# Relative tags early in each fourth step, the second edge bias added by VectorE, the n gate's h half behind the edge transposes

## The reference, cut to what matters

```python
edge_index = jnp.stack([src, dst])
h = jnp.maximum(_layernorm(x, axis=-1), 0.0)
# messages: each edge through the two-layer network of its type
msg_input = jnp.concatenate([h[src], h[dst]], axis=1)
for t in range(n_types):
    a = jax.nn.relu(msg_input @ W1[t] + b1[t])
    m = a @ W2[t] + b2[t]
    msgs = msgs + jnp.where((edge_type == t)[:, None], m, 0)
agg = jax.ops.segment_sum(msgs, dst, num_segments=num_nodes)
# a GRU cell on every node
gi = agg @ W_ih.T + b_ih
gh = h @ W_hh.T + b_hh
r = jax.nn.sigmoid(i_r + h_r)
z = jax.nn.sigmoid(i_z + h_z)
n = jnp.tanh(i_n + r * h_n)
out = x + (1.0 - z) * n + z * h
```

## Time and profile before

| | before |
|---|---|
| median of 3 runs | 1806.55 us (1804.4 to 1809.14) |
| the profiled execution | 1805.01 us, of it 1803.1 in the span |
| TensorE products busy | 1631.5 us (90%) |
| VectorE busy | 1592.3 us (88%) |
| ScalarE busy | 1460.1 us (81%) |
| GpSimd busy | 1235.9 us (69%) |
| TensorE's mean granted clock | 0.98 of full speed |

### The profile page before, as it was taken

How to read it: one execution, slowest core, us unless ns; L and a number is a source line. 1 busy time by engine, 2 the same in 40 slices (tenths; PEclk the granted TensorE clock), 3 DMA queues, 4 the chain that set the end, 5 groups by cost and what they waited for, 6 DMA issues and landing times.

```text
span 1803.1 us, 43100 instructions
## 1 busy us (share of the span) xinstructions
PE 1631.5 (90%) x10182; PEld 1428.9 (79%) x10182; DVE 1592.3 (88%) x4186; ACT 1460.1 (81%) x3401; POOL 1235.9 (69%) x1982
## 2 busy tenths in 40 slices
PE   0226799999999999999999999999999999999998
PEld 0115688888888888888888888888888888888887
DVE  8597699888989898898899999999999999999886
ACT  0025788888888888888888999989989999899895
POOL 4777777777777777777776676666767667676420
PEclk9985899999999999999999999999999999999999
DMA  2224677777777777777777777777777777777653
GB/s 70 50 46 125 166 191 194 195 188 192 193 195 193 194 197 188 188 188 191 193 190 196 195 195 199 193 197 197 196 198 194 199 199 192 200 193 197 182 145 96
DMA packets 477071, 319.72 MB, mean 177 GB/s; under 512 B 106705, under 2 KB 463009, under 8 KB 476962
## 3 DMA queue, kind: packets, MB, share of 16 engines
q10 hardware_dynamic: 261792, 156.12, 28.6%
q1 hardware_dynamic: 185730, 106.99, 25.9%
q0 software_dynamic: 29440, 55.47, 12.8%
HBM read 211.65 MB, written 106.72 MB: 177 GB/s over the span
## 4 chain that ended last, share of the span: by engine, by line
PE 77%; POOL 6%; issue 4%; DVE 2%; ACT 1%; POOLq 0%; ACTq 0%; DVEq 0%
PE bank L1332 14%; PE bank L1334 13%; PE bank L1333 13%; PE bank L1412 10%; PE bank L1424 4%; PE bank L1423 4%; PE bank L1440 4%; PE bank L1450 4%; PE bank L1402 4%; PE bank L1394 4%; POOL e_x L580 3%; DVE n_sel L1071 2%; PE bank L1436 1%; POOL lists L566 1%; ACT e_h L1177 0%
## 5 line engine op out<-in xcount | busy, mean ns | idle before, releaser
L580 POOL DMA_INDIRECT e_x<-in_x,rows_now x816 | 852.5, 1045 | 237.4 <-issue 220.5
L1177 ACT ACTIVATE e_h<-e_x,shift,rstd 128x128 f32<-128x128 f32 x816 | 355.4, 485 | 117.3 <-DVE shift L1048 93.3
L1194 ACT ACTIVATE n_h<-n_x,shift,rstd 128x128 f32<-128x128 f32 x784 | 385.0, 492 | 0.1
L1071 DVE TENSOR_SCALAR n_sel<-iota,n_rel 128x256 fp32r<-128x256 f32 x784 | 233.1, 359 | 37.6 <-POOL n_rel L631 35.7
L1412 PE MATMUL bank<-n_sel,n_win 128*128 128x256 f32 x1568 | 235.0, 292 | 31.0 <-DVE n_sel L1071 31.0
L1332 PE MATMUL bank<-n_h_hi,whh_hi 128*128 128x512 f32 x588 | 247.8, 421 | 2.9 <-ACT n_zc L1285 2.6
L1332 PE MATMUL bank<-n_a_hi,wih_hi 128*128 128x512 f32 x588 | 249.5, 424 | 0.9 <-DVE bank L1083 0.9
L1333 PE MATMUL bank<-n_h_lo,whh_hi 128*128 128x512 f32 x588 | 233.0, 396 | 0.0
L1334 PE MATMUL bank<-n_a_hi,wih_lo 128*128 128x512 f32 x588 | 232.6, 396 | 0.0
L1334 PE MATMUL bank<-n_h_hi,whh_lo 128*128 128x512 f32 x588 | 232.4, 395 | 0.0
L1333 PE MATMUL bank<-n_a_lo,wih_hi 128*128 128x512 f32 x588 | 232.1, 395 | 0.0
(11 more groups left out here) (179 smaller groups left out, 3757.7 us busy)
## 6 DMA issues: line engine op xcount, KB each, us to landing
n_win<-messages SPq DMA_DIRECT2D x1568, 64.2 KB
messages<-e_msg ACTq DMA_DIRECT2D x204, 257.0 KB, 3.1
n_x<-in_x ACTq DMA_DIRECT2D x195, 256.0 KB
out<-n_out ACTq DMA_DIRECT2D x195, 256.0 KB
e_x<-in_x,rows_now POOLq DMA_INDIRECT x816
rows_now<-lists SPq DMA_DIRECT2D x204, 2.0 KB, 3.0
lists<-picks,list_rows POOLq DMA_INDIRECT x72, 2.9
w<-in_W SPq DMA_DIRECT2D x1, 512.0 KB, 4.9
```

The source lines that it names most:

```text
L580: G.indirect_dma_start(e_x[:, s, 2 * end + t, :], None, x, bass.IndirectOffsetOnAxis(ap=rows_now[:, s, t, end:end + 1], axis=0)).then_inc( ...
L1071: ins = V.tensor_scalar(n_sel[:, s % 2, k, :], iota[:], n_rel[:, s % 2, k:k + 1], None, ALU.is_equal)
L1177: last = A.activation(e_h[:, s % 2, k, :], e_x[:, s, k, :], ACT.Relu, scale=rstd[:, slot, col + k:col + k + 1], bias=shift[:, slot, col + ...
L1194: last = A.activation(n_h[:, s % 2, cols], n_x[:, s, cols], ACT.Relu, scale=rstd[:, slot, col + 4 + k:col + 5 + k], bias=shift[:, slot, co ...
```

## The change

Four edits. (1) GpSimd makes `n_rel` in steps with m mod 4 = 2, the ones behind the inverse roots, ahead of the gate and of all four gathers instead of behind the second. (2) TensorE's product of ones with the bias rows goes, and the products with `w2` start the bank themselves. Instead the bias is laid out once over all partitions as `b2_all` (ScalarE copies it in step 7 out of `bank[BIN]`, where an existing product has put it), and VectorE adds it in each step: `e_m` = bank + `b2_all`, behind n_e, for unit i-9. (3) So ScalarE makes the high half from `e_m`, in SBUF, one step later than before (unit i-10), behind the first two `e_h`; VectorE takes `e_m` for the low half; TensorE may overwrite the bank once `e_m` is made (`e_biased`) and not only after the low half. (4) TensorE's h half of the n gate comes behind the edge transposes.

```diff
--- before.py
+++ after.py
@@ -129,6 +129,8 @@
         bneg = sb("bneg", [P, 3])
         b1_cols = sb("b1_cols", [P, TYPES])
         b2_rows = sb("b2_rows", [P, TYPES * D], F32R)
+        b2_all = sb("b2_all", [P, TYPES * D])
+        e_m = sb("e_m", [P, 2 * D])
         row_is = sb("row_is", [P, 2])
 
 
@@ -368,6 +370,9 @@
         e_relued = sem("e_relued")
         e_messaged = sem("e_messaged")
         e_high = sem("e_high")
+        e_biased = sem("e_biased")
+        b2_spread = sem("b2_spread")
+        b2_copied = sem("b2_copied")
         e_low = sem("e_low")
 
 
@@ -671,10 +676,13 @@
                         pool.wait_ge(e_normed, i - 7)
                 if h is not None:
                     wait_half(h)
+                if m % 4 == 2:
+                    relative_tags(i - LAG + 1, m - LAG + 1)
                 transfers_may_start(i + 1 + 2 * TYPES)
                 if within(i, UNITS):
                     gather(i, m, (0,))
-                relative_tags(i - LAG + 1, m - LAG + 1)
+                if m % 4 != 2:
+                    relative_tags(i - LAG + 1, m - LAG + 1)
                 if within(i, UNITS):
                     gather(i, m, (1,))
                 if h is not None:
@@ -1059,7 +1067,7 @@
                 if within(q, UNITS):
                     dve.wait_ge(e_high, q + 1)
                     V.tensor_tensor(e_msg[:, s, :, D:2 * D],
-                                    bank[BE1][:, message_part].rearrange("p (t d) -> p t d", t=2),
+                                    e_m[:].rearrange("p (t d) -> p t d", t=2),
                                     e_msg[:, s, :, 0:D].bitcast(F32), ALU.subtract).then_inc(e_low, 1)
                 ln_part(i, m, 0)
                 g, s = i - LAG + 1, (m - LAG + 1) % 4
@@ -1118,6 +1126,16 @@
                     if due(g - 1):
                         dve.wait_ge(n_back, g - 1)
                     V.tensor_tensor(n_e[:, s, :], n_d[:, s, :], n_zc[:, s, :], ALU.mult).then_inc(n_eed, 1)
+                q = i - 9
+                if within(q, UNITS):
+                    dve.wait_ge(e_messaged, q + 1)
+                    if isinstance(q, int) and q == 0:
+                        dve.wait_ge(b2_copied, 1)
+                    if due(q):
+                        dve.wait_ge(e_low, q)
+                    first = 2 * ((m - 9) % 2)
+                    V.tensor_tensor(e_m[:], bank[BE1][:, message_part], b2_all[:, first * D:(first + 2) * D],
+                                    ALU.add).then_inc(e_biased, 1)
                 ln_part(i, m, 7)
                 if isinstance(i, int) and i == 0:
                     keep_records()
@@ -1234,6 +1252,12 @@
 
             def step(i, m):
                 normalise_edges(i, m, (0, 1))
+                q, s = i - 10, (m - 10) % UNROLL
+                if within(q, UNITS):
+                    act.wait_ge(e_biased, q + 1)
+                    act.wait_ge(e_tagged, q + 1)
+                    A.activation(e_msg[:, s, :, 0:D], e_m[:].rearrange("p (t d) -> p t d", t=2),
+                                 ACT.Copy).then_inc(e_high, 1)
                 g, s = i - LAG, (m - LAG) % 2
                 if within(g, NG):
                     act.wait_ge(n_gate_r, g + 1)
@@ -1285,12 +1309,9 @@
                     A.activation(n_zc[:, s, :], bank[BRZ][:], ACT.Sigmoid, bias=bneg[:, 1:2],
                                  scale=-1.0).then_inc(n_zed, 1)
                 normalise_nodes(i, m, (3,))
-                q, s = i - 9, (m - 9) % UNROLL
-                if within(q, UNITS):
-                    act.wait_ge(e_messaged, q + 1)
-                    act.wait_ge(e_tagged, q + 1)
-                    A.activation(e_msg[:, s, :, 0:D], bank[BE1][:, message_part].rearrange("p (t d) -> p t d", t=2),
-                                 ACT.Copy).then_inc(e_high, 1)
+                if isinstance(i, int) and i == 7:
+                    act.wait_ge(b2_spread, 1)
+                    A.activation(b2_all[:], bank[BIN][:], ACT.Copy).then_inc(b2_copied, 1)
 
             pipeline(nc, act, LAST, LOOP_END, step)
 
@@ -1325,7 +1346,7 @@
                      ).then_inc(s_ranked, 1)
             pe.wait_ge(s_edges_ready, 1)
             pe.wait_ge(s_gates_ready, 1)
-            T.matmul(bank[BIN][:], ones_r[:], b2_rows[:], start=True, stop=True)
+            T.matmul(bank[BIN][:], ones_r[:], b2_rows[:], start=True, stop=True).then_inc(b2_spread, 1)
 
             def product(o, w_hi, w_lo, v_hi, v_lo, start, stop, onto):
                 start = start and not onto
@@ -1380,11 +1401,6 @@
                     if due(g):
                         pe.wait_ge(n_zed, g)
                     gate(BRZ, 0, s, "ha").then_inc(n_gate_r, 1)
-                    if due(g - 1):
-                        pe.wait_ge(n_outed, g - 1)
-                    elif due(g):
-                        pe.wait_ge(n_ted, g)
-                    gate(BHN, 2, s, "h").then_inc(n_gate_hn, 1)
                 q, s = i - 8, (m - 8) % 2
                 if within(q, UNITS):
                     pe.wait_ge(e_normed, q + 1)
@@ -1393,6 +1409,13 @@
                     for k in range(4):
                         last = T.transpose(bank[BE0][:, k * P:(k + 1) * P], e_h[:, s, k, :], ident[:])
                     last.then_inc(e_turned, 1)
+                g, s = i - LAG, (m - LAG) % 2
+                if within(g, NG):
+                    if due(g - 1):
+                        pe.wait_ge(n_outed, g - 1)
+                    elif due(g):
+                        pe.wait_ge(n_ted, g)
+                    gate(BHN, 2, s, "h").then_inc(n_gate_hn, 1)
                 g, s = i - LAG + 1, (m - LAG + 1) % 2
                 if within(g, NG):
                     pe.wait_ge(n_normed, g + 1)
@@ -1416,7 +1439,7 @@
                 if within(q, UNITS):
                     pe.wait_ge(e_evaced, q + 1)
                     if due(q):
-                        pe.wait_ge(e_low, q)
+                        pe.wait_ge(e_biased, q)
                     for t in range(2):
                         o = bank[BE1][:, t * P:(t + 1) * P]
                         kind = 2 * ((m - 9) % 2) + t
@@ -1433,11 +1456,9 @@
                 if within(q, UNITS):
                     pe.wait_ge(e_relued, q + 1)
                     first = 2 * ((m - 9) % 2)
-                    T.matmul(bank[BE1][:, message_part], ones_r[:], b2_rows[:, first * D:(first + 2) * D],
-                             start=True, stop=False)
                     for t in range(2):
                         o = bank[BE1][:, 2 * P + t * D:2 * P + (t + 1) * D]
-                        last = T.matmul(o, e_r[:, s, t * P:(t + 1) * P], w2[:, first + t, :], start=False, stop=t == 1)
+                        last = T.matmul(o, e_r[:, s, t * P:(t + 1) * P], w2[:, first + t, :], start=True, stop=True)
                     last.then_inc(e_messaged, 1)
                 g, s = i - LAG - 1, (m - LAG - 1) % 2
                 if within(g, NG):
```

## The result

The changed kernel takes 1815.37 us (1814.63 to 1818.04, 6 runs) against 1806.67 us before: a ratio of 1.0049, 95% interval 1.0037 to 1.0062. Its profiled execution took 1818.04 us, 1816.1 of it in the span, 13.0 us more than before.

A forecast was written before the change was run, and what follows sets the result against it. TensorE's order of work was taken as the period (8.02 us steps), with a loop through VectorE and ScalarE having 0.35 us spare. From 1805.0 us, -22.2 + 15.5 + 14.0 gave 1812.3, as a median 1813.8; range 1793 to 1833.

The forecast's parts named there:

- n_rel early: GpSimd, step behind the inverse roots: n_rel ahead of two gathers removes TensorE's waits for n_sel outside the head, -22.2 us.
- The product L1436: TensorE's bias product, 0.12 us in each of 194 steps: its 23 us are not gained, TensorE waits for n_sel instead.
- e_m on the loop: VectorE's added 0.34 us operation between n_e and n_sel lengthens steps by 0.08 us on average, +15.5 us (0 to 31).
- h half behind the edge transposes: TensorE's n gate starts 0.32 us later while n_out, which it awaits, ends 0.34 later: 0 us.
- The head: Steps 9 to 14: e_m ahead of VectorE's picks waits for the same step's message products, +14.0 us (2 to 17).
- L1061 and ScalarE's copy: Low half reading e_m from SBUF and ScalarE's high-half copy from SBUF, taken as 0.40 us: no slowdown or lateness, 0 us.
- (a): Rival: the head does not wait, costing 2 instead of 14 us; 1801.8 us, chance 0.15.
- (b): Rival: the loop keeps its spare as the slow n_sel goes away, steady term 0; 1798 us, chance 0.07.
- (c): Rival: TensorE's 23 us from the removed product survive, n_e getting n_zc over 0.3 us earlier; 1775 us, chance 0.05.
- (d): Rival: L1061 or its ScalarE copy late by lock or SBUF latency, 0.1 us each step, +19; 1833 us, chance 0.15.
- (e): Rival: n_rel still late, windows missing or GpSimd full, +11 to +22; 1825 to 1836 us, chance 0.08.
- The first one: Sign: TensorE's n_sel waits 0.1 to 0.35 us in nearly each step; no VectorE n_rel wait over 1 us, 200 to 1700.

The follow-up runs named there:

- edit 1 alone: Kernel before with only n_rel made ahead of the gate and gathers in steps with m mod 4 = 2: 1777.28 us, ratio 0.9823.
- the sum that nobody reads: Kernel before with n_rel early plus an unread 128x256 VectorE sum each step: behind n_e 1819.43 us, behind n_h_lo (off the loop) 1775.98 us.

## Why the prediction was right in the sum and where its steps were not

The time came to 1815.4 us where 1813.8 was forecast, and the steps from the profile's 1805.0 us were -22.2, +15.5 and +14.0. They measured -28.2, +27.5 and +14.1. The total is near in part by luck. The errors of the first two terms, -6.0 and +12.0, cancel by half. The rest, 6 us, shows in the profiled executions, where +13.0 stands against the +7.3 of the sum; between the medians it is +8.7, in part because the profiled execution of the changed kernel was the slowest of its six.

- **n_rel early: -22.2 was mis-sized, measured -28.2** in steps (edit 1 alone), and -29.4 between medians of different series (1806.67 to 1777.28), 32 by the ratio of 0.9823. The mechanism was right: `n_rel` stands ahead of the gathers and VectorE waits for it only in the first group. The step that failed is the row the term was read from. The products' row has 31.0 us of waiting for `n_sel`, the weight loads' 37.3, of which 26.6 went with edit 1.
- **The product L1436: "not gained" was right, its reason only in part.** The prediction let TensorE come 0.12 us earlier to `n_sel` and wait there. It did not come earlier: the r gate waits for n_zc, which keeps its place behind the z gate, and with the loop relieved the 23 us do not come either. No sentence of the prediction had that wait.
- **e_m on the loop: +15.5 was mis-sized, measured +27.5** (steps of 1593.0 against 1565.5 with edit 1 alone). The mechanism was right. The step with the root's seed got longer by 0.26 us for 0.23 forecast, and it holds the waits for `n_sel`: 48 of the 53 by the weight loads, 12.4 us. The reading of the timeline gave 0.11 us a step, and I went down to 0.08 for the earlier part with no row for it. It came to 27.5 / 195 = 0.14, and to 0.15 in the first 88 steps against 0.13 in the later ones. What the forecast had too low were the other three steps, with some 0.1 each (0.07 in the mean of them forecast). They make up half of the 27.5 us, and no wait by name stands for them; that they go with the low half off the loop says that they belong to it. The 0.35 that I read at `n_sel` was the spare of one closing only. In the order of before the tighter one was n_out to the h half, with 0.11; in the changed kernel the moved gate had given it room.
- **h half behind the edge transposes: 0 was the wrong size, it is worth 21 us** (18.4 in the steps) beside `e_m`, and nothing measurable without `e_m` (1775.2 and 1773.9). The prediction had the two numbers (0.32 and 0.34) and saw that they match; it did not ask what the second would cost without the first. All of `e_m` on the loop in the old order is +45.9 us (steps 1611.4 against 1565.5), near the +43.4 of the sum that nobody reads; the moved gate brings that back to 27.5. So the sum's +15.5 and 0 are right in company only: the edit that was put at nothing carries part of the other.
- **The head: +14.0 was right, measured 14.1.** The five waits are 2.04 to 2.90 us, 11.8 together, for 2.2 to 2.9 and some 12 forecast, and the first `n_sel` starts at 206.7 for "near 206".
- **L1061 and ScalarE's copy: 0 was right.** The low half L1069 with both inputs in SBUF has a median of 417 ns against 416 before, and a longest of 512 against 425; the lock that the Trainium skill ("SBUF — State Buffer", Who interferes with whom) could let one expect is not seen in the median. VectorE waited for the copy 3.4 us in 6 cases.

Of the rivals, (a), (b), (c) and (d) did not come true: the head waited, the loop kept no spare, TensorE's 23 us did not survive, the copy was in time. For (e), one wait of 5.8 us for `n_rel` is all that is left. Added up as the prediction says, its chances for slower, within and faster come to about 0.56, 0.24 and 0.20, not 0.55, 0.28 and 0.17.

Of the signs, the steady step (1593.0 / 195 = 8.17 us) and the head came as forecast. The first one came only in part: TensorE waits for `n_sel` in about one step of four, not in nearly each.

The profile calls the r gate's wait "issue". That it is for n_zc rests on three things: the program waits for it there, the weights start 0.04 to 0.13 us behind n_zc's end in practically every step, and the product put back, in two kernels, fills the wait at no cost. With edit 1 alone the weights follow n_zc as closely, in 194 of 194 steps, so of its 8.02 us some 1.0 is the stretch from the z gate's end over n_zc to the r gate (622.00 to 623.01). Whether a shorter n_zc would shorten the step was not tried, and no run takes the bias product out of the kernel before by itself.

The best kernels of this study are edit 1 alone and its neighbours with the low half behind `n_sel`: 1773.9 to 1777.3 us, 1.8 to 1.9% faster than before and 2.1 to 2.3% faster than the changed kernel. Of the whole change edit 1 is all that pays on its own.

## What to carry to other kernels

Before an operation is added to an engine that is not the bound, find the loop that runs through it and the bound engine, and every place where that loop closes; the spare is that of the tightest one, and an operation off the loop may cost nothing where the same one on it costs 43 us. Before work is taken from the bound engine, look at what waits for time to pass behind it: a result's reader (here n_zc, between two gates on one bank) can hold the engine just as long. Look for TensorE's waits in its weight loads, since its products' rows overlap and hide short ones. But take the price from the starts, of the products or of the steps: 73.0 us of idle weight loads cost 43.4 us here.

## What the runs showed of the hardware

- The rows of the products hide short waits, and those of the weight loads overstate them. With the added operation on the loop the weight loads ahead of the h half sat idle for 73.0 us in 186 cases, the products ahead of it for 0.3 us in one, and the steps grew by 43.4 us. The mean of the first pass went from 421 to 456 ns there, with the gate in its old place.
- The first pass of a gate lasts 0.40 us behind another product of 512 columns and 0.48 behind transposes (624.51 before, 1105.67 after), without a wait.
- The r gate's first weight load starts 0.04 to 0.13 us behind the end of n_zc, whose bank it writes, in 190 of 190 steps before.
- ScalarE's copy of 128x256 takes 418 ns out of SBUF (`e_m`) and 371 ns out of PSUM: the forecast had 0.40 us. The row before stands there, the row after is

```profile
L1259 ACT ACTIVATE e_msg<-e_m x204: 416/418/423, 125.8 to 1791.6; 128x256 fp32r<-128x256 f32 x102
```
